# A gated scan with four token-state products per chunk: transpositions cut into row halves, the key projection moved ahead, and VectorE's order to suit

## What is computed

```python
def step(carry, xs):
    W_in, W_out = carry
    qi, ki, vi, li, lo, wi, wo = xs
    p_q = softmax(einsum('bnhd,bDhd->bnhD', qi, W_in), axis=1)   # over the chunk's tokens
    o = einsum('bnhD,bDhd->bnhd', p_q, W_out)
    p = softmax(einsum('bnhd,bDhd->bnhD', ki, W_in), axis=1)
    grad_out = einsum('bnhD,bnhd->bDhd', -p, vi)
    a = einsum('bDhd,bnhd->bnhD', W_out, vi)
    s = sum(p * a, axis=-1)
    g_z = -(p * a - p * s)
    grad_in = einsum('bnhd,bnhD->bDhd', ki, g_z)
    W_in = wi * W_in - li * grad_in
    W_out = wo * W_out - lo * grad_out
    return (W_in, W_out), o
```

## Time and profile before

| | us |
|---|---|
| median of three runs | 1089.22 |
| the three runs | 1084.87, 1089.22, 1090.20 |
| the profiled execution | 1082.43 |
| its span, first to last instruction | 1080.6 |
| busy in the span: PE, DVE, POOL, ACT | 784.5, 772.3, 611.5, 471.7 |

### The profile page before, as it was taken

How to read it: one execution, slowest core, us unless ns; L and a number is a source line. 1 busy time by engine, 2 the same in 40 slices (tenths; PEclk the granted TensorE clock), 3 DMA queues, 4 the chain that set the end, 5 groups by cost and what they waited for, 6 DMA issues and landing times. The chain is left out here.

```text
span 1080.6 us, 33735 instructions
## 1 busy us (share of the span) xinstructions
PE 784.5 (73%) x14259; PEld 708.1 (66%) x14261; DVE 772.3 (71%) x1084; ACT 471.7 (44%) x640; POOL 611.5 (57%) x408
## 2 busy tenths in 40 slices
PE   4084623783699999999999999999999971615720
PEld 2042623672588899888889898999999861604620
DVE  3864572563498899899898998998898856481107
ACT  2431401220656556566557557475646433202312
POOL 2302305533176878778687887868687871204524
PEclk9667556997799999999999999999999995557865
DMA  7233301231005000000000000000000001502236
GB/s 189 65 77 115 114 0 41 64 62 47 15 5 163 5 8 5 5 8 5 8 6 8 5 5 6 2 3 3 3 3 2 4 3 50 146 0 57 62 96 154
DMA packets 67503, 43.89 MB, mean 41 GB/s; under 512 B 22036, under 2 KB 62120, under 8 KB 67240
## 3 DMA queue, kind: packets, MB, share of 16 engines
q1 hardware_dynamic: 64040, 35.05, 12.2%
q0 software_dynamic: 3328, 6.82, 2.7%
HBM read 27.70 MB, written 14.16 MB: 39 GB/s over the span
## 5 line engine op out<-in xcount | busy, mean ns | idle before, releaser
L1513 PE MATMUL psum<-hT,w_qkv 128*128 128x128 f32 x1536 | 186.6, 278 | 9.3 <-ACT hT L693 9.3
L482 POOL TENSOR_TENSOR arena<-arena 128x1024 f32<-128x1024 f32 x64 | 121.5, 1898 | 118.7 <-PE psum L1546 118.7
L1513 PEld LDWEIGHTS psum<-hT,w_qkv 128*128 128x128 f32 x1536 | 178.7, 193 | 11.3 <-issue 7.2
L512 POOL TENSOR_TENSOR arena<-arena,small 128x1024 f32<-128x1024 f32 x64 | 122.2, 1911 | 24.5 <-DVE small L1144 24.3
L496 POOL TENSOR_TENSOR arena<-arena 128x1024 f32<-128x1024 f32 x64 | 121.6, 1900 | 0.0
L1137 DVE TENSOR_REDUCE small<-arena 128x16 f32<-128x1024 f32 x64 | 77.5, 1211 | 0.6 <-ACT arena L725 0.6
L1126 DVE TENSOR_REDUCE small<-psum 128x16 f32<-128x1024 f32 x64 | 77.5, 1213 | 0.6 <-PE psum L1605 0.6
L516 POOL TENSOR_TENSOR arena<-arena 128x1024 f32<-128x1024 f32 x32 | 75.1, 2348 | 3.3 <-DVE arena L1158 3.3
L469 POOL DMA_INDIRECT arena<-h_rows,route x40 | 40.0, 1001 | 65.2 <-issue 44.1
L705 ACT ACTIVATE arena<-psum 128x1024 f32<-128x1024 f32 x32 | 33.0, 1032 | 99.6 <-PE psum L1513 99.6
L1132 DVE TENSOR_TENSOR arena<-psum,small 128x1024 f32<-128x1024 f32 x64 | 75.0, 1214 | 0.0
(11 more groups left out here) (284 smaller groups left out, 1809.1 us busy)
## 6 DMA issues: line engine op xcount, KB each, us to landing
h_rows<-arena SPq DMA_DIRECT2D x8, 512.0 KB, 3.2
y_rows<-hT SPq DMA_DIRECT2D x8, 512.0 KB, 7.1
arena<-y_rows SPq DMA_DIRECT2D x8, 512.0 KB, 7.2
o_rows<-arena SPq DMA_DIRECT2D x10, 256.0 KB
x_sb<-in_L_attn_u SPq DMA_DIRECT2D x8, 256.0 KB, 5.9
arena<-in_W_inT SPq DMA_DIRECT2D x16, 128.0 KB, 2.6
arena<-in_W_out SPq DMA_DIRECT2D x64, 32.0 KB, 2.2
arena<-in_L_ffn_W SPq DMA_DIRECT2D x8, 256.0 KB, 2.7
```

The costliest lines, as they stand in the source:

```text
L482: pool.tensor_tensor(w4, w4, d4.unsqueeze(3).to_broadcast([P, 2, HP, D]), ALU.mult).then_inc(done, 1)
L512: pool.tensor_tensor(z4, z4, r3.unsqueeze(3).to_broadcast([P, 8, 2, CH]), ALU.mult).then_inc(done, 1)
L1513: mm = pe.matmul(ps[bank][:, p * P:(p + 1) * P], w_qkv[:, j * HD + p * P:j * HD + (p + 1) * P], hT[:, at:at + P], start=True, stop=True)
```

## The change

Four things change in the scan.

- The transpositions of `k_turn`, `p_turn` and `v_turn` are made in halves: where one transposition took 128 partitions by 128 columns and a unit matrix of 128, two now take 64 partitions by 128 columns each and a unit matrix of 64. 8 instructions become 16, and each pair lies on the two row halves of the array. Their outputs lie in another order, which the copies on ScalarE put right (`by_pairs`, `by_halves`).
- `states_q` makes o alone, with 64 moving columns. W_out is transposed by 16 half transpositions of its own (`states_turn`) into ps[2], once `k_tok_out` has read ps[2].
- The projection of the keys stands right behind the query's, ahead of `grad_in` and `k_turn`.
- On VectorE, `add_up(i-1, 0)` and `q_silu(i)` stand ahead of `update_in(i-3)`. ScalarE's and GpSimd's order stays.

The head order of W_out's columns changes with it, in the DMAs that load it and in the host's layout of the rates. The diff, without the new semaphore's declaration, the same edit in `v_tok_out`, `p_tok_out`, `grad_out` and `v_turn`, and the host's line:

```diff
@@ -317,7 +317,7 @@
-                                sp.dma_start(w_out[bp][q * D:(q + 1) * D, half].rearrange("d (g r j c) -> d g r j c", g=2, r=2, c=D)[:, g, r],
+                                sp.dma_start(w_out[bp][q * D:(q + 1) * D, half].rearrange("d (g j r c) -> d g r j c", g=2, r=2, c=D)[:, g, r],
                                              A["W_out"].rearrange("(g j e r) d c -> g e r d j c", g=2, e=2, r=2)[g, q ^ r, r]
...
             def k_tok_out(t):
                 act.wait_ge(pe_kt, t + 1)
                 after(act, pe_gin, t)
-                act.activation(k_tok, ps[2], ACT.Copy).then_inc(ktok_out, 1)
-
-            def of_states(k):
-                return psum[:, 0:2048].rearrange("r (g k c) -> r k g c", k=2, c=D)[:, k]
+                act.activation(by_pairs(k_tok), by_halves(ps[2]), ACT.Copy).then_inc(ktok_out, 1)
+            def by_pairs(x):
+                return x.rearrange("r (p k d) -> r k p d", k=2, d=D)
+
+            def by_halves(x):
+                return x.rearrange("r (k p d) -> r k p d", k=2, d=D)
 
             def w_outT_out(t):
-                act.wait_ge(pe_ow, t + 1)
+                act.wait_ge(pe_wt, t + 1)
                 after(act, pe_a, t)
-                act.activation(w_outT.rearrange("r (g c) -> r g c", c=D), of_states(1), ACT.Copy).then_inc(woutT_out, 1)
+                act.activation(w_outT, ps[2], ACT.Copy).then_inc(woutT_out, 1)
 
             def oT_of(t):
                 act.wait_ge(pe_ow, t + 1)
                 after(act, pe_y, t)
-                act.activation(oT.rearrange("r (g c) -> r g c", c=D), of_states(0), ACT.Copy).then_inc(oT_out, 1)
+                act.activation(oT, ps[0], ACT.Copy).then_inc(oT_out, 1)
...
@@ -1200,12 +1203,12 @@
                     group_measure(i // 4 + 2)
                 if i >= 0 and i % 4 == 1 and i // 4 + 2 < NC:
                     group_rate(i // 4 + 2)
+                if 0 <= i + 2 < T:
+                    add_up(i + 2, 0)
+                if 0 <= i + 3 < T:
+                    q_silu(i + 3)
                 if 0 <= i < T:
                     update_in(i)
-                if 0 <= i + 3 < T:
-                    q_silu(i + 3)
-                if 0 <= i + 2 < T:
-                    add_up(i + 2, 0)
                 if 0 <= i + 3 < T:
                     k_silu(i + 3)
...
+            def turn_halves(out, of, at):
+
+                for n in range(HP):
+                    for r in range(2):
+                        mm = pe.transpose(out[:, col((r, 2), (n, HP))], of[half(r), at(n):at(n) + P], eye[half(r), :])
+                return mm
+
+            def states_turn(t):
+                for j in range(4):
+                    for be in range(2):
+                        for q in range(2):
+                            at = (be * 8 + 2 * j) * D
+                            mm = pe.transpose(ps[2][:, col((q, 2), (j, 4), (be, 2))], w_out[t % BP][half(q), at:at + P], eye[half(q), :])
+                mm.then_inc(pe_wt, 1)
+
             def states_q(t):
                 for j, e, be, r, q, p, s in pairs(range(4)):
-                    at = zs_at + 2048 * (t % 2) + s * 256 + be * D
-                    o_and_eye = arena[half(q), at:2 * eye_at - at].rearrange("r (k x) -> r k x", k=2)[:, :, 0:D]
-                    mm = pe.matmul(ps[2 * q][half(r), (j * 2 + be) * P:(j * 2 + be + 1) * P].rearrange("r (k n) -> r k n", k=2),
-                                   w_out[t % BP][half(q), col((be, 2), (s, 8))], o_and_eye, start=True, stop=True)
+                    at = s * 256 + be * D
+                    mm = pe.matmul(ps[0][half(r), col((q, 2), (j, 4), (be, 2))], w_out[t % BP][half(q), col((be, 2), (j, 4), (r, 2))],
+                                   zs[t % 2][half(q), at:at + D], start=True, stop=True)
...
             def k_turn(t):
                 pe.wait_ge(silu_k, t + 1)
-                for p in range(HP):
-                    mm = pe.transpose(ps[2][:, p * P:(p + 1) * P], qk[t % 2][:, 1024 + p * P:1024 + (p + 1) * P], ident[:, :])
-                mm.then_inc(pe_kt, 1)
+                turn_halves(ps[2], qk[t % 2], lambda p: 1024 + p * P).then_inc(pe_kt, 1)
...
             def p_turn(t):
-                for r in range(2):
-                    for j in range(4):
-                        at = slot(r, j) * 256 + P
-                        mm = pe.transpose(ps[3][:, (4 * r + j) * P:(4 * r + j + 1) * P], zs[t % 2][:, at:at + P], ident[:, :])
-                mm.then_inc(pe_pt, 1)
+                turn_halves(ps[3], zs[t % 2], lambda n: slot(n // 4, n % 4) * 256 + P).then_inc(pe_pt, 1)
...
@@ -1643,6 +1652,9 @@
                     if c and i % 4 == 3:
                         pe.wait_ge(group_rates, c + 1)
                     project(i, 0, 1, pe_pq)
+                if i < T:
+                    after(pe, z_centered, 2 * i)
+                    project(i, 1, 3, pe_pk)
...
                         pe.wait_ge(oT_out, i - 2)
                         pe.wait_ge(woutT_out, i - 2)
                     k_turn(i - 2)
-                if i < T:
-                    after(pe, z_centered, 2 * i)
-                    project(i, 1, 3, pe_pk)
                 if i == 0:
                     group_sum(0)
                 if 2 <= i < T + 2:
+                    pe.wait_ge(ktok_out, i - 1)
+                    after(pe, wout_new, i - 5)
+                    states_turn(i - 2)
                     pe.wait_ge(pq_norm, i - 1)
                     after(pe, vT_out, i if i == 2 else 0)
                     after(pe, win_new, i - 2)
-                    pe.wait_ge(ktok_out, i - 1)
-                    after(pe, wout_new, i - 5)
                     states_q(i - 2)
```

## The result

The changed kernel takes **1126.06 us** (median of 4 runs, 1124.89 to 1130.97), the one before 1087.05 (4 runs, 1080.93 to 1090.20): a ratio of **1.036 [1.032, 1.040]**, slower. The forecast was 1114, with 1092 to 1132 as its range. The profiled execution took 1126.25 (span 1124.4), against 1082.43 (span 1080.6) before.

A forecast was written before the change was run, and what follows sets the result against it. TensorE was taken to bound the kernel before, a loop of waits the changed one. Six groups at +3.1 us and five plain rounds at +1.45, less about 1, gave +25: 1114 us at the median, range 1092 to 1132.

The forecast's parts named there:

- The half turn at 0.6: On TensorE, a transposition made in halves was taken to last 0.6 us, against 0.93 to 1.02 for a full one.
- The middle price by weight loads, 0.84: On TensorE, a half turn would take 0.84 us if loading 128 weight columns sets its time.
- the high end, 1.68: On TensorE, a half turn would take 1.68 us if its two row halves don't overlap.
- The states at 1.69: On TensorE, `states_q` at 1.82 us becomes 0.6 for W_out's turn plus 1.09 for 32 products: 1.69.
- The loop of 19.06: From centring through key projection, `grad_in`, `k_turn`, `k_tok_out`, exponentials, `k_tanh`, `k_silu` to next centring: 19.06 us against 17.61, +1.45 a round.
- 0.75 of slack: TensorE's own list from `k_silu` to the next key projection takes 11.6 us, where VectorE allows 12.4: 0.75 us spare.
- The group extras, 2.6 instead of 5.3: Extra work per group of four rounds, partly covered by VectorE's new idle time: 2.6 us instead of 5.3.
- The clock stays at 1.00, since new pauses are 1.2 at most: TensorE's granted clock in the scan was to stay at its full level, the new pauses being 1.2 us at most.
- The last rounds, -1: The scan's last rounds, without projections, have shorter turns: about 1 us less in total.
- VectorE binds and nothing stalls: Rival: VectorE becomes the bound, 29 rounds at -1.5 us give -43, 1046 us at the median; chance 8%.
- Weight loads set the half turns: Rival: each half turn on TensorE takes 0.84 us, giving 1121 us; chance 18%.
- Half turns don't overlap, or the clock falls: Rival: turns of 1.68 us make TensorE's round about 22, some 1220 us, or its clock drops to 1.2 GHz; chance 4%.

The follow-up runs named there:

- e2_order_only: The kernel before with full turns and only the two orders changed (key projection on TensorE, VectorE's order): ratio 1.055 to the kernel before, 1143.76 us.
- e1_half_turns: The kernel before with only the half turns, `states_turn` and output copies of the change, both orders as before: ratio 0.990 to the kernel before, 1075.74 us.
- e3_ktok_behind: The changed kernel with `k_tok_out` moved behind the exponentials and `k_tanh` on ScalarE: ratio 1.040 to the kernel before, 1126.72 us.
- e13_two_k_tok: The changed kernel with `k_turn` ahead of `grad_in` and two `k_tok` tiles used in turn instead of one: ratio 1.031 to the kernel before.
- e10_turn_first: The changed kernel with `k_turn` ahead of `grad_in` on TensorE, still one `k_tok` tile: ratio 1.036 to the kernel before.
- e12_turn_first_take_earlier: The changed kernel with `k_turn` ahead of `grad_in` and `group_take` one round earlier: ratio 1.035 to the kernel before.
- e5_old_dve: The changed kernel with VectorE's old order put back, all else as changed: ratio 1.026 to the kernel before, 1104.63 us.
- e6_take_late: The changed kernel with `group_take` moved behind `update_in` on VectorE: ratio 1.029 to the kernel before, 1103.60 us.
- e8_take_earlier: The kernel before with half turns and split states, both orders as before, and `group_take` one round earlier: ratio 0.986 to the kernel before, 1058.12 us.
- e4_half_new_dve: The changed kernel with the key projection put back behind `k_turn`; half turns and VectorE's new order stay: ratio 1.010 to the kernel before, 1096.46 us.
- e7_three_half_turns: The kernel before with half turns for k, p and v only, `states_q` in one and both orders as before: ratio 0.995 to the kernel before, 1067.21 us.
- e11_logits_in_two: The kernel before with the logits' 64 products of 128 moving columns made as 128 of 64: ratio 1.015 to the kernel before, 1089.07 us.

## Why the prediction was right, and where it was not

- **TensorE bounds the kernel before, and a loop could outlast it**: right. TensorE's busy time fell, and the kernel became slower.
- **The half turn at 0.6**: it is 0.64 (838.20 to 838.84). The middle price by weight loads, 0.84, and the high end, 1.68, are refuted. Its loads last 134/138/226 ns (least, median, most), as those of full turns did; the line is below. By the Trainium skill's rule for loads ("TensorE: Matmul & The Clock Gate", section "LDWEIGHTS") a turn would have taken 0.85, an estimate of the prediction; the measurement decides against it for turns.
- **The states at 1.69**: `states_turn` and `states_q` take 1.62 (838.20 to 839.82). Right.
- **The loop of 19.06**: measured 18.85, and each link stands in the trace. Centring to key projection 2.40 (2.41 said), to `grad_in` 1.98 (1.88), to `k_turn` 1.10 (1.09), to `k_tok_out` 0.75 (0.80), to `k_silu` 2.91 (2.92), to the next centring 9.71 (9.96). The last is 0.25 less than said: with the wait for `a_of` taken off, the round that it was read from still had small gaps between VectorE's instructions which this one hasn't. The waits are there as forecast: 0.93 for `grad_in` (0.85), 2.31 for `k_tanh` (2.5), 1.12 for `k_tok_out` (1.2), 0.40 for `centre`. `e2_order_only` shows that the order makes the loss, and `e1_half_turns` that the half turns make none.
- **The loop is the only cause**: incomplete. The prediction gave TensorE's list 0.75 of slack and let it go. That the two loops are nearly of one length is shown by `e3_ktok_behind`: to cut the first alone gives nothing. As a forecast of this change it did no harm; as a guide to a repair it failed in `e3_ktok_behind` and `e13_two_k_tok`, while `e10_turn_first` and `e12_turn_first_take_earlier` failed by the one `k_tok` tile.
- **The group extras, 2.6 instead of 5.3: the step that failed.** The sum had 29 x 1.45 = 42 from the loop less 16 from extras. Measured are 36.0 from the loop and +1.5 from extras, so this one term is 17.7 off, in part made up by the loop's 6. That the total came out near, 1126 against 1114, is in part luck: the two errors have opposite signs. The take round costs 2.79 over a plain one, not 1.1. I had seen that `group_take` delays `update_in`, `states_q` and `grad_out`, and not that the wait for it falls beside the 1.12 that the loop itself makes. The hT round (1.08) and the other two (0.38 and 0.88) are above the 0.6 and 0.9 of the forecast as well.
- **The clock stays at 1.00, since new pauses are 1.2 at most**: wrong, and about half of that miss. Take rounds with a fall last 1.3 more than the one without, rate rounds 1.1 more than those without: 8 us in seven rounds. The prediction sized each pause alone. Even its own example, 1.32, did not stand alone: 1.11 stood ahead of `grad_in`, with 2.2 us of work between, and the next products still ran at full pace:

```profile
863.29 1.16 PE L1560 MATMUL psum<-arena 64*64 64x64 f32 x64 [1.11 <-ACT arena L705]
```

- `e5_old_dve` and `e6_take_late` take away the wait for `update_in`, keep the clock, and bring take rounds down by 1.7 and 1.6. Between the first and the last centring they are 7.0 and 10.6 us shorter. What else is in the miss was not taken apart; TensorE's stops for "issue" rose too, to 9.6 us in 18 from 310 to 850, against 5.1 in 10.
- **The last rounds, -1**: not shown. The stretch behind the last centring is 1.0 shorter, but `e1_half_turns` and `e8_take_earlier`, whose last rounds are the same, have 218.6 and 220.1 there, so 1.0 says nothing.
- **The rivals.** "VectorE binds and nothing stalls" would need TensorE and ScalarE without waits; TensorE has 53.9 us of them from 310 to 850, where it had 12.8. "Weight loads set the half turns" gave 1121, nearer to 1126 than my own figure, by a mechanism that the trace refutes: a near number is no evidence for it. "Half turns don't overlap, or the clock falls" is half true in its second part, at a price of some 8 us where I had only thought of the whole scan.

**Open.** Where TensorE's stops for "issue" fall, and why in one round and not in the next, no run tells. Nor does one tell why the clock falls behind two pauses in one round and not behind the same two in another. How the 1.040 of `e3_ktok_behind` divides between the second loop, such stops and a lowered clock in its group rounds, was not taken apart, nor whether the difference of `e5_old_dve` and `e6_take_late` over the scan, between first and last centring (601.6 and 598.0, against 608.6) means anything.

## What to carry to other kernels

When an order is moved, walk every loop that goes through the moved step, also the one through the bound engine's own list and back, and write down the length of each: cutting the longest is worth no more than its distance to the next. A copy that a turn feeds has two conditions, its source and the tile that it overwrites. And where pauses come to stand close together on TensorE, don't say that the clock holds because each of them is short: read it in windows of a few us behind them.

## What the runs showed of the hardware

- **Pauses that stand together on a busy TensorE can halve its clock, and need not.** Kept in all plain rounds of the changed kernel: 0.20 to 0.40 and 1.12, with 3.8 us of work between (64 products in 1.16). Lost: 1.12 and 1.35 around 0.71 of work (1.75 and 2.01), 0.46, 0.31 and 1.12 (1.89 and 1.95), 2.59 alone in `e4_half_new_dve` (1.75 and 2.00). Either way: 1.20 and 1.27 in `e10_turn_first`. Kept again: 2.74 alone in `e13_two_k_tok` (468.74, 1.16). A fall cost 1.5 to 1.6 us in the durations of the next 128 products, and the page's tenths show nothing of it.
- **Two row halves of a turn overlap.** 16 transpositions of 64x128 with 64 moving columns take 0.64 us, where 8 of 128x128 take 0.93; and with four such turns a round the clock is 1.00 in eleven stretches of 40 us of `e1_half_turns` and of `e5_old_dve`. Their weight loads are no shorter than those of a full turn:

```profile
L1549 PEld LDWEIGHTS psum<-arena x1536: 134/138/226, 304.7 to 931.1; 64*128 64x128 f32 x192
```

- **Kernels with more TensorE instructions had more stops that the profile puts down to no engine, but not in proportion.** From 310 to 850 us, one execution each: 5.1 us in 10 for the kernel before (33735 instructions of all engines), 5.1 in 13 for `e2_order_only` (33736), 10.2 in 12 for `e7_three_half_turns` (35272), 9.6 in 18 for the changed kernel (36295), 12.6 in 25 for `e1_half_turns` (36296), 8.5 in 17 for `e11_logits_in_two` (37832). The kernels with half turns have more stops than the number of instructions explains.
